# A recurrent scan with mixture-of-experts routing: where row scatters wait, how many expert tiles are known early, and when their outputs are summed

## The chip, the cores and the metric

The kernel runs on one core of one Trainium2 chip. The metric is the device time of one execution in microseconds (us), the median of several runs. A core has five engines that run their own instruction streams and meet only at semaphores: TensorE (PE in the profile; PEld is its weight load), VectorE (DVE), ScalarE (ACT), GpSimd (POOL) and SyncE (SP), which here only issues transfers.

## What is computed

Two blocks on x, of shape (32, 128, 128): batch, time, features.

```python
h = scan(h*(1-alpha) + sigmoid(h@Wh.T + z_t@Wz.T + b)*z_t -> tanh)      # gated scan over 128 steps
x = x + attention(h)                                                    # 16 heads, relative embeddings
h_t = tanh(x_t @ Wx + b + h_{t-1} @ Wh)                                 # second scan over 128 steps
p = softmax(h @ router_w.T); w, idx = top_k(p, 2); w = w / (w.sum() + 1e-9)
out = sum_k w_k * (gelu(h @ w1[idx_k].T + b1[idx_k]) @ w2[idx_k].T + b2[idx_k])
x = x + out                                                             # 8 experts, hidden width 512
```

The change concerns the second scan, the routing and the experts. Each of the 4096 tokens (32 x 128) goes to two of eight experts.

## The kernel before

After the first scan and the attention comes a block that runs the second scan, the routing and the experts.

**The scan.** The 128 steps are cut into NCH = 8 chunks of TC = 16. Iteration m of `chunks` scans chunk m and routes chunk c = m - 1. In step j TensorE waits for the state before (s_h2), multiplies it by Wh (`column_products`, 8 instructions at L420, raising s_r) and then does side work: input sums of the next chunk, the output projection, router logits (steps 5, 9, 13 and 1 of the next chunk), the states' rows (steps 2 to 5) and positions (step 7). ScalarE waits for s_r and takes the tanh (L1125), raising s_h2. This is a closed ring of two engines.

**The routing.** From logits and positions VectorE finds for each token and choice a slot in a list sorted by expert (`choose`, `state_rows`, `slots`, `weights`) and raises s_slot. GpSimd then scatters the rows of the chunk to their slots in the tensor expert_inputs: 2 x JT = 8 indirect transfers (k = 0 to 7) of 128 rows each (L1195 in `scatter`). `scatter_step(c, k)` is the step of the scan at which transfer k of chunk c is due; before each, GpSimd waits for `scatter_step(c, k) + 1` on s_h2, which starts at 1, so for the state of the step ahead. Transfers whose step lies behind the scan (chunk 6, k = 3 to 7: `behind_scan`) and the eight of chunk 7 are issued between expert tiles, at the tiles that `scatter_tiles` names: 0 to 4, and 8, 9, 11, 12, 14, 15, 17, 18.

**The tiles.** The sorted list is worked off in NS = 71 tiles of 128 rows. SyncE loads a tile's rows (`load`, L948, eight buffers RX, each free again when the tile eight before has been written back). TensorE turns them (`turn`, L1079), VectorE copies the columns (L1421), TensorE multiplies by the expert's first weights (`up`, L1086), ScalarE applies the gelu (L1143), TensorE multiplies by the second weights (L1107), VectorE adds the bias (L1471), and GpSimd scatters the tile's 128 output rows to expert_outputs (L1203). ScalarE (L1152) and VectorE (L1427) copy the expert's weights ahead. Sums are double buffered.

Which expert a tile belongs to comes from a table. The first NA = 3 * RX = 24 tiles are full and known from the counts after CA = 4 chunks: VectorE's `early_table(0)`, (1), (2) run behind the routing of chunks 3, 4 and 5, and TensorE's `table_rows(0)` in step 13 of the iteration that routes chunk 5. The others follow from all counts (`late_table`, during tiles 8 to 13). Before SyncE loads tile NA it waits until every row scatter has landed. The first UNROLLED = 24 tiles are written out, the others run in a loop of eight on TensorE, ScalarE and GpSimd.

**The sum over choices.** From tile COMBINE = 44 on VectorE adds, in each tile, one piece (`combine`, two instructions at L1439) of a chunk's two weighted choices to the residual rows; four pieces are a chunk. SyncE loads a chunk's outputs (L957) behind `load(loaded_behind(c))` and stores the finished rows (L961) behind `load(stored_behind(c))`. Pieces that are left when the tiles end run behind the last tile, then chunk 7's weights and its own sum.

Of the kernel before, what the change touches and what calls it, by code (L numbers as in the profile page):

```python
# [14 lines left out]
T = 128  # L15
# [25 lines left out]
def build(nc, a):  # L41

    with ExitStack() as ctx:
# [794 lines left out]
        RX = 8  # L839
        CA = 4  # L840
        NA = 3 * RX
        NB = NS - NA
# [35 lines left out]

        UNROLLED = SPREAD + RX

        def over_tiles(eng, step, late=None):
            for i in range(UNROLLED // RX):
                if late and i == SPREAD // RX:
                    late()
                for k in range(RX):
                    step(i, k, i * RX + k, True, True)
# [11 lines left out]
        s_out = sem("output_written")  # L898
        COMBINE = 44

        def loaded_behind(c):

            return max(tiles_until(c) - 1 + RX, COMBINE + 2 + 2 * c)

# [3 lines left out]

        assert all(COMBINE + JT * c >= loaded_behind(c) - RX + 6 for c in range(NCH - 1))

# [5 lines left out]
        def scatter_step(c, k):  # L916

            return (c + 1) * TC + 10 + 2 * k

        behind_scan = [(NCH - 2, k) for k in range(2 * JT) if scatter_step(NCH - 2, k) >= T]  # L920
        scatter_tiles = dict(enumerate(behind_scan))
        scatter_tiles.update((RX + k + k // 2, (NCH - 1, k)) for k in range(2 * JT))
        assert len(behind_scan) < RX and scatter_step(NCH - 3, 2 * JT - 1) < T

        with nc.Block() as block:
            @block.sync
            def _(sp):
# [12 lines left out]
                for o in range(2):  # L940
                    sp.wait_ge(s_sc[o], CA // 2 * 16 * 2 * JT)

# [51 lines left out]
            def _(pe):  # L994

                def step(m, scan_on, route_on):
# [5 lines left out]
                    for j in range(TC):  # L1002
# [44 lines left out]
                        if j == 7 and scan_on:  # L1047
                            positions(c, 4, 0)
                        if j == 13 and scan_on and c == CA + 1:
                            table_rows(0)  # L1050
# [124 lines left out]
            def _(pool):  # L1175
# [5 lines left out]
                def step(m, scan_on, route_on):  # L1181
# [6 lines left out]
                    for k in range(2 * JT):  # L1188
                        if scatter_step(c, k) < T:
                            pool.wait_ge(s_h2, scatter_step(c, k) + 1)  # L1190
                            scatter(c, k)
# [24 lines left out]
            def _(dve):  # L1216
# [155 lines left out]
                def step(m, scan_on, route_on):  # L1372
# [10 lines left out]
                    for part in range(3):  # L1383
                        slots(c, 4, 0, part)
                    weights(c)
                    count(begun[:, c + 1, :], 0, ALU.is_gt, lambda op: link(c, op))
                    assert k[0] == VLINKS, k
                    if CA - 1 <= c < CA + 2:
                        early_table(c - CA + 1)
                    if m == 1:  # L1390
# [147 lines left out]
```

## Time and profile before

| what | us |
|---|---|
| median of 3 runs | 727.92 |
| lowest, highest | 723.27, 728.98 |
| the profiled execution, whole | 724.73 |
| its span on the core | 721.8 |
| TensorE busy | 600.0 (83%) |
| VectorE busy | 433.5 (60%) |
| GpSimd busy | 400.9 (56%) |
| ScalarE busy | 392.9 (54%) |

Times in the rows are counted from the start of the span; "us" after the start is the length. In square brackets stands how long the engine had been idle and what ended that.

### The profile page before, as it was taken

How to read it: one execution, taken by the hardware profiler on the slowest of the kernel's cores; microseconds unless marked ns; L12 is line 12 of the kernel's file. 1: busy time of each engine (PE TensorE's matmuls, PEld its weight loads, DVE VectorE, ACT ScalarE, POOL GpSimd, SP SyncE). 2: the span in 40 equal slices, each digit the busy share in tenths (PEclk: the TensorE clock that was granted, in tenths of full speed). 3: DMA queues.
4: the chain of work that ended last, by engine and by line, in shares of the span. 5: the costliest groups of instructions: out<-in, count | busy, mean ns of one | idle time of the engine just before them, and what ended most of it. 6: DMA issues, size and time to landing. Idle time of an engine off the chain costs nothing. (4 is left out here: it accounts for less than half of the span.)

```text
span 721.8 us, 27264 instructions
## 1 busy us (share of the span) xinstructions
PE 600.0 (83%) x10479; PEld 454.4 (63%) x10479; DVE 433.5 (60%) x2041; ACT 392.9 (54%) x1112; POOL 400.9 (56%) x433
## 2 busy tenths in 40 slices
PE   3888888888879989999997857777777788999993
PEld 1565555555667766776675734334445777999993
DVE  1666666666557677677765334555545553456775
ACT  4666666666414545555553523222225656899893
POOL 4445554445338878798777421545443656565552
PEclk9999999999979999999999988555556989999997
DMA  7356655555686766677666024333111222225452
GB/s 254 118 207 228 226 186 210 206 205 196 236 246 186 221 177 184 163 217 199 178 182 208 3 88 152 102 97 102 36 54 32 62 79 68 75 75 175 133 160 98
DMA packets 111943, 108.69 MB, mean 151 GB/s; under 512 B 7136, under 2 KB 85472, under 8 KB 111440
## 3 DMA queue, kind: packets, MB, share of 16 engines
q1 hardware_dynamic: 107120, 97.66, 43.0%
q0 software_dynamic: 4320, 8.89, 3.7%
q8 instruction: 78, 1.28, 0.8%
q10 hardware_dynamic: 384, 0.52, 0.2%
q14 instruction: 41, 0.34, 0.2%
HBM read 59.43 MB, written 45.52 MB: 145 GB/s over the span
## 5 line engine op out<-in xcount | busy, mean ns | idle before, releaser
L515 POOL TENSOR_TENSOR sc<-sc,mx 128x1024 f32<-128x1024 f32 x64 | 121.2, 1899 | 53.2 <-DVE mx L673 53.2
L406 POOL TENSOR_SCALAR QD<-q_all,mask 128x128 f32<-128x128 f32 x126 | 88.8, 717 | 98.0 <-DVE pre L361 94.9
L673 DVE CUSTOM_DVE_ANT_0 sc<-banks,s2t 128x128 f32<-128x128 f32 x512 | 112.0, 286 | 49.6 <-PE banks L566 48.2
L1203 POOL DMA_INDIRECT expert_outputs<-yr,xr x71 | 78.5, 1106 | 67.1 <-DVE yr L1471 33.8
L731 ACT ACTIVATE PT<-banks 128x512 f32<-128x512 f32 x128 | 69.8, 596 | 64.2 <-PE banks L579 64.2
L1195 POOL DMA_INDIRECT expert_inputs<-rows,slotu x64 | 63.5, 992 | 68.5 <-ACT h L1125 49.6
L1143 ACT ACTIVATE hid<-banks,w1b 128x128 f32<-128x128 f32 x284 | 81.0, 368 | 24.6 <-PE banks L1086 17.7
L352 DVE COPY s2stage<-banks 128x512 f32<-128x512 f32 (+1 forms) x90 | 76.6, 852 | 16.5 <-PE banks L253 16.5
L1125 ACT ACTIVATE h<-banks,bias 128x32 f32<-128x32 f32 x128 | 36.8, 288 | 86.4 <-PE banks L420 80.2
L1086 PE MATMUL banks<-xt,w1b 128*128 128x128 f32 x568 | 78.0, 282 | 6.8 <-DVE xt L1421 6.8
L1107 PE MATMUL banks<-w2b,hid 128*128 128x128 f32 x568 | 78.4, 283 | 5.3 <-ACT hid L1143 4.9
L253 PE MATMUL banks<-RK,QD 32*128 32x128 f32 x1024 | 78.5, 454 | 3.9 <-DVE s2stage L352 0.9
L1086 PEld LDWEIGHTS banks<-xt,w1b 128*128 128x128 f32 x568 | 71.3, 197 | 8.4 <-DVE xt L1421 8.4
L1107 PEld LDWEIGHTS banks<-w2b,hid 128*128 128x128 f32 x568 | 71.6, 198 | 6.9 <-ACT hid L1143 5.9
L579 PEld LDWEIGHTS banks<-ident,sc 128*128 128x128 f32 x512 | 56.4, 143 | 28.8 <-issue 13.9
L579 PE MATMUL banks<-ident,sc 128*128 128x128 f32 x512 | 70.9, 283 | 0.0
L219 PEld LDWEIGHTS banks<-hs,wh 128*32 128x32 f32 x1016 | 25.5, 140 | 71.2 <-ACT hs L312 71.2
L420 PEld LDWEIGHTS banks<-h,wh 128*32 128x32 f32 x1016 | 24.8, 133 | 71.7 <-ACT h L1125 54.9
L361 DVE TENSOR_TENSOR_SCAN pre<-xz,gl 128x64 f32<-128x64 f32 x128 | 37.5, 293 | 53.9 <-ACT gl L309 50.7
L420 PE MATMUL banks<-h,wh 128*32 128x32 f32 x1016 | 41.1, 242 | 32.0 <-ACT h L1125 27.6
L253 PEld LDWEIGHTS banks<-RK,QD 32*128 32x128 f32 x1024 | 61.1, 318 | 9.8 <-issue 7.8
L219 PE MATMUL banks<-hs,wh 128*32 128x32 f32 x1016 | 42.6, 251 | 28.9 <-ACT hs L312 25.5
(144 smaller groups left out, 1062.7 us busy)
## 6 DMA issues: line engine op xcount, KB each, us to landing
s_scratch<-s2stage SPq DMA_DIRECT2D x32, 1024.0 KB, 4.8
s2t<-s_scratch SPq DMA_DIRECT2D x64, 512.0 KB, 4.9
xr<-expert_inputs SPq DMA_DIRECT2D x71, 64.5 KB
xz<-in_xz SPq DMA_DIRECT2D x8, 512.0 KB, 5.7
yb<-expert_outputs SPq DMA_DIRECT2D x16, 256.0 KB
w2all<-in_w2b SPq DMA_DIRECT2D x8, 320.0 KB
w1a<-in_w1b SPq DMA_DIRECT2D x8, 258.0 KB
k_all<-in_xT SPq DMA_DIRECT2D x1, 2048.0 KB, 11.2
```

The lines of the kernel that those rows point to most:

```text
L219: mm = pe.matmul(ps[bank][at, lo:hi], w[:, at], moving, start=first, stop=last, tile_position=(0, 32 * c), skip_group_check=True)
L253: mm = pe.matmul(ps[4 + j][:, tl * T:(tl + 1) * T], QD[G % 3][32 * j:32 * j + 32, tl].rearrange("p h b -> p (h b)"), relk_window(j, t), st ...
L352: dve.tensor_copy(stage[G % SETS][:, lo:hi].rearrange("p g q k -> p (g q k)"), banks[:, (4 + lo) * BANK:(4 + hi) * BANK]).then_inc(s_s2c, 1)
L406: op = pool.tensor_scalar(QD[G % 3][:, :, h, :], q_all[:, :, quad(G)].rearrange("p b t -> p t b"), mask[:, h:h + 1], None, ALU.mult)
L515: pool.tensor_tensor(sc[U % RING][:], sc[U % RING][:], mx[U % RING][:].unsqueeze(2).broadcast_to([P, HH, T]), ALU.subtract)\
L579: mm = pe.transpose(blocked[:, j // 2, j % 2], sc[U % RING][:, 4 * x + j, :], ident[:])
L673: op = dve.tensor_tensor_reduce(out=sc[r][:, h, :], in0=ps[2 * (U % 2) + h // 4][:, h % 4 * T:(h % 4 + 1) * T], in1=s2t[r][:, h, :], scale ...
L731: act.activation(pairs[:, 2 * (2 * u + x):2 * (2 * u + x) + 2], ps[4 + x][:].rearrange("p (a r) -> p a r", a=2), ACT.Exp, scale=DH ** -0.5 ...
L1086: mm = pe.matmul(ps[2 + k % 2][:, f * P:(f + 1) * P], w1b[k % 2][:, f * P:(f + 1) * P], xt[k % 2][:], start=True, stop=True)
L1107: mm = pe.matmul(ps[4 + k % 2][:, 0:D], hid[k % 2][:, f, :], w2b[k % 2][:, f * D:(f + 1) * D], start=(f == 0), stop=(f == FC - 1))
L1143: op = act.activation(hid[k % 2][:, f, :], ps[2 + k % 2][:, f * P:(f + 1) * P], ACT.Gelu, bias=w1b[k % 2][:, FF + f:FF + f + 1])
L1203: pool.indirect_dma_start(yg_dram, bass.IndirectOffsetOnAxis(xr[k][:, D:].bitcast(U32), 0), yr[k][:], None).then_inc(s_ys[k], 16)
```

## The change

- CA goes from 4 to 5 and NA from 24 to 32: the early table is made from five chunks and covers 32 tiles. `early_table(0)` moves behind chunk 4, (1) into the routing of chunk 5 between slots and weights, (2) behind it; `table_rows(0)` moves to step 15 of that iteration. SyncE's first wait for row scatters counts five chunks.
- UNROLLED goes from 24 to 32 tiles; ScalarE's wait for the late table stays eight tiles ahead of its end.
- `scatter_step` is one step later (11 + 2k), and the wait is for s_r, the product of that step, instead of s_h2.
- The 13 scatters behind the scan go to tiles 1, 2, 4, 5, 7, 9, 11, ..., 23.
- COMBINE goes from 44 to 50, and with it the tiles at which outputs are loaded (54, 54, 56, 58, 60, 62, 70 instead of 46, 48, 50, 52, 54, 62, 70) and sums stored.

```diff
--- before.py
+++ after.py
@@ -837,8 +837,8 @@
         WEIGHTS_IN = 2 * 16 * E
         VLINKS = 20
         RX = 8
-        CA = 4
-        NA = 3 * RX
+        CA = 5
+        NA = 4 * RX
         NB = NS - NA
         ALINKS = 7
         TLINKS = 16
@@ -876,11 +876,11 @@
         s_w2r = sem("second_weights_ready")
         s_tpass = sem("gpsimd_tile_wait_passed")
 
-        UNROLLED = SPREAD + RX
+        UNROLLED = SPREAD + 2 * RX
 
         def over_tiles(eng, step, late=None):
             for i in range(UNROLLED // RX):
-                if late and i == SPREAD // RX:
+                if late and i == UNROLLED // RX - 1:
                     late()
                 for k in range(RX):
                     step(i, k, i * RX + k, True, True)
@@ -896,7 +896,7 @@
         s_o0 = sem("first_choice_added")
         s_sum = sem("chunk_summed")
         s_out = sem("output_written")
-        COMBINE = 44
+        COMBINE = 50
 
         def loaded_behind(c):
 
@@ -906,7 +906,7 @@
 
             return COMBINE + JT * (c + 1) + RX - 2
 
-        assert all(COMBINE + JT * c >= loaded_behind(c) - RX + 6 for c in range(NCH - 1))
+        assert all(COMBINE + JT * c >= loaded_behind(c) - RX + 4 for c in range(NCH - 1))
 
         def fill(eng, e):
 
@@ -915,12 +915,12 @@
 
         def scatter_step(c, k):
 
-            return (c + 1) * TC + 10 + 2 * k
+            return (c + 1) * TC + 11 + 2 * k
 
         behind_scan = [(NCH - 2, k) for k in range(2 * JT) if scatter_step(NCH - 2, k) >= T]
-        scatter_tiles = dict(enumerate(behind_scan))
-        scatter_tiles.update((RX + k + k // 2, (NCH - 1, k)) for k in range(2 * JT))
-        assert len(behind_scan) < RX and scatter_step(NCH - 3, 2 * JT - 1) < T
+        left_over = behind_scan + [(NCH - 1, k) for k in range(2 * JT)]
+        scatter_tiles = dict(zip((1, 2, 4, 5, 7, 9, 11, 13, 15, 17, 19, 21, 23), left_over, strict=True))
+        assert scatter_tiles[9] == (NCH - 1, 0) and scatter_step(NCH - 3, 2 * JT - 1) < T
 
         with nc.Block() as block:
             @block.sync
@@ -938,7 +938,7 @@
 
                 sp.wait_ge(s_tab, ALINKS)
                 for o in range(2):
-                    sp.wait_ge(s_sc[o], CA // 2 * 16 * 2 * JT)
+                    sp.wait_ge(s_sc[o], (CA + 1 - o) // 2 * 16 * 2 * JT)
 
                 def load(t):
                     i, k = t // RX, t % RX
@@ -1046,7 +1046,7 @@
                                     rows_of(k)
                         if j == 7 and scan_on:
                             positions(c, 4, 0)
-                        if j == 13 and scan_on and c == CA + 1:
+                        if j == 15 and scan_on and c == CA:
                             table_rows(0)
 
                 def states(r, k):
@@ -1187,7 +1187,7 @@
                     pool.wait_ge(s_slot, c + 2)
                     for k in range(2 * JT):
                         if scatter_step(c, k) < T:
-                            pool.wait_ge(s_h2, scatter_step(c, k) + 1)
+                            pool.wait_ge(s_r, scatter_step(c, k) + 1)
                             scatter(c, k)
 
                 def scatter(c, k):
@@ -1382,11 +1382,15 @@
                         state_rows(c, 3, part)
                     for part in range(3):
                         slots(c, 4, 0, part)
+                    if c == CA:
+                        early_table(1)
                     weights(c)
                     count(begun[:, c + 1, :], 0, ALU.is_gt, lambda op: link(c, op))
                     assert k[0] == VLINKS, k
-                    if CA - 1 <= c < CA + 2:
-                        early_table(c - CA + 1)
+                    if c == CA - 1:
+                        early_table(0)
+                    if c == CA:
+                        early_table(2)
                     if m == 1:
                         dve.wait_ge(s_xrow, 16)
                         add_rows(0)
```

## Rows read from the trace of the kernel before

**Rows 1.** Busy time by stretch: the second scan, early tiles, later tiles.
```profile
core 0: us, PE busy (x) PEld busy (x) DVE busy (x) ACT busy (x) POOL busy (x), PEclk, DMA share, GB/s
432.00:552.00 120.00, 88.97 (x2291) 48.44 (x2291) 63.17 (x321) 37.95 (x132) 52.78 (x54) 0.57 0.29 90
552.00:620.00 68.00, 57.01 (x450) 53.83 (x448) 32.67 (x122) 44.12 (x126) 37.80 (x36) 0.91 0.25 64
620.00:710.00 90.00, 87.75 (x780) 87.02 (x779) 59.16 (x192) 80.85 (x230) 51.86 (x47) 1.00 0.42 124
```

**Rows 2.** Chain of waits, 425 to 500 us, shares by engine and line.
```profile
by line: PE banks L420 66.5%; ACT h L1125 15.4%; issue 6.0%; DMA packed<-in_packed 6.0%; another core or an unknown queue 2.5%
```

**Rows 3.** Timeline of ScalarE ahead of the first scatter: start, length, instruction, idle before.
```profile
446.43 0.29 ACT L1125 ACTIVATE h<-banks,bias 128x32 f32<-128x32 f32 x1 [0.39 <-PE banks L420]
447.10 0.29 ACT L1125 ACTIVATE h<-banks,bias 128x32 f32<-128x32 f32 x1 [0.39 <-PE banks L420]
```

**Rows 4.** Timeline of all engines in the scan, steady scatters.
```profile
490.66 0.96 POOL L1195 DMA_INDIRECT expert_inputs<-rows,slotu  x1 [1.03 <-ACT h L1125]
...
490.84 0.29 ACT L1125 ACTIVATE h<-banks,bias 128x32 f32<-128x32 f32 x1 [0.45 <-PE banks L420]
...
491.18 0.33 PE L420 MATMUL banks<-h,wh 128*32 128x32 f32 x8
...
492.00 0.29 ACT L1125 ACTIVATE h<-banks,bias 128x32 f32<-128x32 f32 x1 [0.88 <-PE banks L420]
...
492.57 0.96 POOL L1195 DMA_INDIRECT expert_inputs<-rows,slotu  x1 [0.95 <-ACT h L1125]
```

**Rows 5.** All row scatters: length in ns, shortest, median, longest.
```profile
L1195 POOL DMA_INDIRECT expert_inputs<-rows,slotu x64: 957/960/1472, 447.8 to 609.9; - x64
```

**Rows 6.** Timeline of all engines: the first three scatters of a chunk.
```profile
480.00 0.96 POOL L1195 DMA_INDIRECT expert_inputs<-rows,slotu  x1 [1.46 <-ACT h L1125]
...
480.02 0.33 PE L420 MATMUL banks<-h,wh 128*32 128x32 f32 x8
...
480.60 0.29 ACT L1125 ACTIVATE h<-banks,bias 128x32 f32<-128x32 f32 x1 [0.63 <-PE banks L420]
...
481.21 0.69 DVE L1227 TENSOR_TENSOR x1r<-x1r,packed 128x512 f32<-128x512 f32 x1
481.26 1.47 POOL L1195 DMA_INDIRECT expert_inputs<-rows,slotu  x1 [0.30 <-issue]
482.81 0.29 ACT L1125 ACTIVATE h<-banks,bias 128x32 f32<-128x32 f32 x1 [1.93 <-remote]
...
483.56 0.29 ACT L1125 ACTIVATE h<-banks,bias 128x32 f32<-128x32 f32 x1 [0.46 <-PE banks L420]
...
484.12 0.96 POOL L1195 DMA_INDIRECT expert_inputs<-rows,slotu  x1 [1.38 <-ACT h L1125]
485.41 0.29 ACT L1125 ACTIVATE h<-banks,bias 128x32 f32<-128x32 f32 x1 [1.57 <-PE banks L420]
```

**Rows 7.** Timeline of all engines: scatters in a run, early tiles.
```profile
559.42 0.96 POOL L1195 DMA_INDIRECT expert_inputs<-rows,slotu  x1 [0.30 <-issue]
...
560.69 0.96 POOL L1203 DMA_INDIRECT expert_outputs<-yr,xr  x1 [0.30 <-issue]
...
561.95 0.96 POOL L1195 DMA_INDIRECT expert_inputs<-rows,slotu  x1 [0.31 <-issue]
...
563.80 1.14 ACT L1143 ACTIVATE hid<-banks,w1b 128x128 f32<-128x128 f32 x4 [1.86 <-remote]
...
564.22 1.16 PE L1086 MATMUL banks<-xt,w1b 128*128 128x128 f32 x8 [1.61 <-DVE xt L1421]
```

**Rows 8.** Chain of waits in order of time: the last row scatter's landing.
```profile
609.93 2.35 DMA expert_inputs<-rows,slotu
```

**Rows 9.** Timeline of VectorE behind the last tile.
```profile
710.19 0.73 DVE L1439 SCALAR_TENSOR_TENSOR x1r<-yb,wts,x1r 128x128 f32<-128x128 f32 x2
...
717.20 2.44 DVE L1439 SCALAR_TENSOR_TENSOR x1r<-yb,wts,x1r 128x128 f32<-128x128 f32 x8 [4.99 <-DMA yb<-expert_outputs]
```

## Prediction

> **What bounds the kernel now.** I read the busy time by stage first [rows 1]. The change touches three stages: the second scan (432 to 552 us), the expert tiles while GpSimd still scatters routed rows (552 to 620), and the remaining tiles with the sum over choices (620 to 710). The scan is not short of an engine: TensorE shows 89 of 120 us, but at a granted clock share of 0.57, so mostly at 1.2 of its 2.4 GHz. Its 128 steps take 120 us, 0.94 us each. The chain of waits over its first half [rows 2] says what a step is: TensorE's product (L420), then the tanh on ScalarE (L1125), then the next product. So the scan ends when 128 round trips have ended, and anything that makes one trip longer is paid in full.
>
> How long is a trip when nothing disturbs it? Before the first scatter, two states in a row start 0.67 us apart, ScalarE idle 0.39 between them [rows 3], although TensorE has its side work there too. Once scatters run, the steady pattern is another [rows 4]: a scatter starts at 490.66; the state at 490.84 comes on time (idle 0.45, a trip of 0.74 at the lower clock); its successor's product starts at 491.18, yet its state starts only at 492.00, 0.82 behind the product where 0.40 is normal (490.84 less 490.44, the product's start one 0.74 trip earlier). The product is held for 0.42 us. The next scatter comes at 492.57, so two trips take 1.91 instead of 1.48: 0.43 per scatter. The scatter itself lasts 0.96 [rows 5].
>
> At the beginning of a chunk it is worse [rows 6]. Scatter one starts at 480.00, and the product that starts 0.02 later is turned into a state at 480.60, 0.58 behind instead of 0.40: held 0.18. Scatter two is already released and follows 0.30 behind, 481.26 to 482.73; the state after 480.60 comes at 482.81, 2.21 later where 0.74 is normal: held 1.47. Scatter three at 484.12 holds the next one, 485.41 less 483.56 being 1.85: held 1.11. With five steady ones the chunk loses 0.18 + 1.47 + 1.11 + 5 x 0.43 = 4.9 us, against 16 trips of 0.74 = 11.8. That sum, 16.7, is near the spacing of the chunks.
>
> In the tiles one period is 1.91 us: 47 output scatters in 90 us with TensorE busy 87.75 [rows 1]. There TensorE is the bound and nothing is to be won. Between 552 and 620 GpSimd issued 36 scatters, 13 of them routed rows, so 23 tiles were finished in 68 us; 23 x 1.91 is 44, so 24 us are lost, some 5 of them filling the pipeline. Where they go: output and row scatters in a run [rows 7]. Three of a run of four stand there, 559.42, 560.69, 561.95, each 0.30 behind the last (the fourth, an output scatter, ran just ahead of them); ScalarE gets its next sums only at 563.80, 0.9 after the run, and TensorE, out of work, restarts at 564.22 after 1.61 idle. As in the scan, TensorE's finished work is learned of late while GpSimd issues. The stretch's clock, 0.91, costs up to 0.09 x 68 = 6 more. The gate in front of tile 24 shows last: the last row scatter is issued at 609.93 and takes 2.35 to land [rows 8], but it was due at tile 18 and GpSimd was itself behind by then, so I put the gate alone at about 1 us.
>
> **The change, part by part.** (1) The wait of the scan's scatters. Their count stays: steps 11 + 2k instead of 10 + 2k leave the same three of chunk 6 inside the scan, 51 in all. Before, a scatter waited for the state of the step ahead of its own and started 0.27 after that state's end, 0.56 after its start. Now it waits for its step's product, whose signal also starts the state; with the same 0.27 latency it starts about 0.25 after the state's start. The state takes 0.29 and the next product starts 0.05 behind it, 0.34 behind the state's start. So the product at risk starts about 0.09 after the scatter, where it started 0.22 before (passing) and 0.52 after (held) in [rows 4]. The nearest row for +0.09 is the first scatter of a chunk, +0.02, held 0.18 [rows 6]. The following product would start at 0.09 + 0.74 + 0.2 = 1.0, behind the scatter's end at 0.96. I take 0.25 per scatter: bounds 0 (it slips through) and 0.9 (held to where the held ones are let go, 492.00 - 490.66 = 1.34 after the scatter's start, against 0.49 undisturbed). Steady ones gain 5 x (0.43 - 0.25) = 0.9 per chunk.
>
> The first of a chunk cannot start before its slots are known; that is about where it starts today. The second now waits for a product two steps on, some 1.7 us behind the first's start, so it starts some 0.7 us behind the first's end instead of 0.30. The collision goes, and the third's with it: 0.18 + 1.47 + 1.11 - 3 x 0.25 = 2.0 per chunk. Together 2.9 per chunk; 51 scatters are 6.4 chunks: 18.6. Not every chunk is as bad as the one in [rows 6], so I take 16. Behind the waiting scatter only other scatters are queued on GpSimd; their readers (SyncE's loads) come far later.
>
> The SBUF page of the Trainium skill (Who interferes with whom) says that only the port pair shared by VectorE and GpSimd causes contention, TensorE and ScalarE never waiting on anyone. The second scatter of [rows 6] agrees with its other half (1.47 long under a two-input VectorE operation at 481.21, against 0.96), the 0.42 of [rows 4] does not; by the rule alone part (1) is worth nothing.
>
> (2) Table after five chunks. The same VectorE operations, in three other places; the table's product moves from step 13 to 15 of iteration 6. Its values are now computed in that same iteration: about ten small operations of 0.2 to 0.4 us behind the slots. If they are late, TensorE waits in the chain, at most about 1 us once. The first tiles are loaded some 2 us later, 13 us ahead of their use. I take 0.
>
> (3) 32 tiles ahead of the gate, row scatters to tile 23. The gate is then passed eight tiles behind the last row scatter, 15 us against 2.35 for landing: it costs nothing, 1 us won. The spreading wins less than it seems. GpSimd needs 37 issues for tiles 0 to 24 either way; from tile 5 on it is three issues in two tiles, 3 x (0.96 + 0.30) = 3.78 against 2 x 1.91 = 3.82: no gap is left, and runs form again. Fewer pairs stand close (1, 2, 4, 5 at the start, none later, where 8, 9, 11, 12, 14, 15, 17, 18 were). I take one or two stalls of 1.6 fewer less a new one, net 2 won. Bounds: 8 lost (a stall of 1.6 every fourth issue, with no rest in tiles 5 to 7 as before) and 14 won (all but the fill and the low clock). Unrolled code for 32 instead of 24 tiles: TensorE, ScalarE and GpSimd fetch it while they run; 0.
>
> (4) Combination from tile 50. Six more combination steps lie behind the last tile. Each is 0.73 [rows 9], 4.4 us; VectorE sits idle 4.99 there waiting for the last outputs, so they fit with 0.6 to spare. If the cover were gone they would cost those 4.4. At its start chunk 0's outputs are loaded four tiles ahead instead of six: 3.8 us less; VectorE may wait up to 1 us at tile 50. I take 0, range 0 to 2.
>
> Sum: -16 (scan), -1 (gate), -2 (spread) = -19 us. The profiled execution took 724.7 us with a span of 721.8; the median of the runs is 727.9, 3.2 higher. Against the median this gives 709.
>
> **Rivals.** *A, the hold per scatter does not depend on where it starts.* For it: held products appear in nearly every pair. Against it: 490.84 on time and 480.60 late by only 0.18. Then only the collisions go, 1.47 + 1.11 + 0.18 - 3 x 0.43 = 1.5 per chunk at most, and as all chunks are not alike about 6; with 3 from the tiles, -9: 719. *B, slower: the product that starts just behind a scatter is held for the whole issue.* For it: 482.81 and 485.41 [rows 6], let go only about 1.3 to 1.5 after their scatter's start. The price is 0.9 instead of 0.43 for 36 steady scatters (17) less what is saved at the collisions (2.76 - 2.7, nothing): +17 - 3 = +14: 742. It decides from a hold of about 0.68 per scatter: 51 x (0.68 - 0.62, today's mean 4.9 / 8) cancels the 3 us of the tiles. *C, the tiles become one unbroken run.* For it: the 3.78 against 3.82 above. Then (3) costs 8, and with 8 to 16 won in the scan the whole is about -4: 724. *D, the scan by the skill's rule:* nothing in part (1), -3 from the tiles: 725. Against it stands the 0.42.
>
> **How the numbers follow.** Forecast 0.50 (range 700 to 717), A 0.17, B 0.17, C 0.10, D 0.06. About 1%, 7 us, is what a measurement can tell from no change. Faster by more: nearly all of the forecast, most of A, a little of C: 0.64. Within 1%: 0.17. Slower: B and a little of C: 0.19. The range, 699 to 734, leaves out the worse half of B and the tail of the forecast, where the clock would rise too: at the upper level a trip is 0.67 and not 0.74, up to 9 us more.
>
> **What would show it.** Right: the 120 us of the scan near 104; scatters starting about 0.25 behind a state's start; states in a chunk without a gap of 1.9. Wrong: ScalarE idle 1.3 behind every scatter (B). For the tiles: SyncE no longer waits for row scatters; GpSimd's issues 0.30 apart over tiles 5 to 23 with TensorE stalls of 1.6 between them say C. For the end: VectorE's idle time behind the last tile falls from 4.99 to about 0.6.

## The result and the profile after

| | kernel before | changed kernel |
|---|---|---|
| median, us | 725.06 (719.49 to 728.98, 12 runs) | 728.55 (725.76 to 732.21, 12 runs) |
| ratio, 95 % interval | 1 | 1.0075 (1.0055 to 1.0095) |
| profiled execution, whole / span | 724.73 / 721.8 | 728.32 / 726.1 |

The change makes the kernel 0.75 % slower, 3.5 us, where 709 us was forecast: 16 us below the median of the kernel before in this table, 19 below the 727.9 that the forecast started from. The busy time by stretch has the same columns and the same stretches as [rows 1].

```profile
432.00:552.00 120.00, 83.71 (x2202) 46.36 (x2194) 62.77 (x320) 35.09 (x127) 48.85 (x52) 0.57 0.27 84
552.00:620.00 68.00, 55.98 (x484) 50.95 (x484) 31.91 (x118) 42.63 (x120) 35.59 (x35) 0.94 0.23 62
620.00:710.00 90.00, 87.36 (x765) 86.98 (x766) 54.24 (x173) 80.34 (x230) 50.93 (x46) 0.98 0.40 119
```

In the scan's 120 us the trace shows 2202 matmuls of TensorE where it showed 2291: the scan has slowed down. The two tile stretches hardly differ. How long the scan is can be read from the line of its states (first and last start of the 128 tanh instructions), here of the kernel before and of the changed one:

```profile
L1125 ACT ACTIVATE h<-banks,bias x128: 287/288/288, 428.2 to 549.6; 128x32 f32<-128x32 f32 x128
```
```profile
L1125 ACT ACTIVATE h<-banks,bias x128: 287/287/288, 426.7 to 552.5; 128x32 f32<-128x32 f32 x128
```

121.4 us before, 125.8 after: 4.4 us lost where 16 were to be won. What happened to a single scatter is read as in [rows 4], from the timeline of ScalarE, TensorE and GpSimd. First the pattern that is now the commonest, of the changed kernel:

```profile
492.09 0.29 ACT L1125 ACTIVATE h<-banks,bias 128x32 f32<-128x32 f32 x1 [0.45 <-PE banks L420]
...
492.33 0.96 POOL L1195 DMA_INDIRECT expert_inputs<-rows,slotu  x1 [1.32 <-PE banks L420]
492.43 0.34 PE L420 MATMUL banks<-h,wh 128*32 128x32 f32 x8
...
493.67 0.29 ACT L1125 ACTIVATE h<-banks,bias 128x32 f32<-128x32 f32 x1 [1.18 <-PE banks L420]
...
494.41 0.29 ACT L1125 ACTIVATE h<-banks,bias 128x32 f32<-128x32 f32 x1 [0.46 <-PE banks L420]
```

The scatter starts 0.24 behind its state and the product at risk 0.10 behind the scatter, as the prediction worked out (0.25 and 0.09). But this product's state starts only at 493.67, 1.24 behind it and 1.34 behind the scatter: held 0.84. It isn't the data of the transfer that stands in the way. By stretch (columns as in [rows 1]: the scatter's own 0.96 us, then until the state starts, then the next 0.63), the DMA engines move nothing before the state has started:

```profile
492.33:493.29 0.96, 0.86 (x23) 0.31 (x16) 0.67 (x2) 0.16 (x2) 0.96 (x1) 0.50 0.00 0
493.29:493.67 0.38, 0.00 (x0) 0.00 (x0) 0.38 (x2) 0.00 (x1) 0.00 (x0) 0.50 0.00 0
493.67:494.30 0.63, 0.29 (x12) 0.29 (x16) 0.49 (x3) 0.29 (x1) 0.00 (x0) 0.50 0.32 105
```

The same kernel also shows the case that was forecast:

```profile
507.01 0.29 ACT L1125 ACTIVATE h<-banks,bias 128x32 f32<-128x32 f32 x1 [0.46 <-PE banks L420]
507.25 0.96 POOL L1195 DMA_INDIRECT expert_inputs<-rows,slotu  x1 [1.41 <-PE banks L420]
507.35 0.34 PE L420 MATMUL banks<-h,wh 128*32 128x32 f32 x8
...
507.86 0.29 ACT L1125 ACTIVATE h<-banks,bias 128x32 f32<-128x32 f32 x1 [0.56 <-PE banks L420]
...
508.68 0.29 ACT L1125 ACTIVATE h<-banks,bias 128x32 f32<-128x32 f32 x1 [0.54 <-PE banks L420]
```

Same 0.10, held 0.11 and then 0.08, two trips in 1.67. In 42 of the scan's scatters the product starts 0.10 to 0.12 behind: 25 are held 0.80 to 0.95, 16 at most 0.16, one 0.56. Which of the two comes goes for the most part by the scatter's place in its chunk: the fourth is held long in all six chunks, the second and third in none of eleven cases (the 0.56 is one of these), the fifth in three of six. Two more traces with the same wait, e1 and r1 below, show the fourth held in all twelve chunks, the second and third in two of 22. So the distance of 0.10 alone does not say what a scatter costs.

The next table sorts the 127 distances between two successive states of each trace and sums what each class has above 0.74, the undisturbed trip at the lower clock:

| distance, us | before: count, excess | changed: count, excess |
|---|---|---|
| up to 0.8 | 75, -1.1 | 64, -1.1 |
| 0.8 to 1.1 | 9, 1.4 | 29, 3.6 |
| 1.1 to 1.4 | 33, 15.3 | 6, 3.6 |
| 1.4 to 1.9 | 6, 6.0 | 26, 22.8 |
| over 1.9 | 4, 5.9 | 2, 2.9 |

The 33 holds of 0.46 on the mean and most collisions are gone. In their place stand 29 light ones and 26 of about 0.88. The sum of the excess is 27.4 before and 31.8 after; the difference is the 4.4 us. (Two distances in each trace, 0.6 and 1.1 us of excess, stand ahead of the first scatter.) Split by place in the chunk, the two halves of the forecast come apart: the stretches of a chunk's first three scatters, seven in all, have 14.4 us of excess before and 8.7 after, and a steady scatter costs 0.45 before and 0.77 after. The collisions gave 5.7 us, the 30 steady scatters took 9.6.

The first three scatters of one chunk, of the changed kernel, answer to [rows 6]:

```profile
482.69 0.29 ACT L1125 ACTIVATE h<-banks,bias 128x32 f32<-128x32 f32 x1 [0.45 <-PE banks L420]
482.69 0.96 POOL L1195 DMA_INDIRECT expert_inputs<-rows,slotu  x1 [1.91 <-PE banks L420]
...
484.03 0.29 ACT L1125 ACTIVATE h<-banks,bias 128x32 f32<-128x32 f32 x1 [1.05 <-PE banks L420]
484.27 0.96 POOL L1195 DMA_INDIRECT expert_inputs<-rows,slotu  x1 [0.62 <-PE banks L420]
...
484.92 0.29 ACT L1125 ACTIVATE h<-banks,bias 128x32 f32<-128x32 f32 x1 [0.61 <-PE banks L420]
...
485.77 0.29 ACT L1125 ACTIVATE h<-banks,bias 128x32 f32<-128x32 f32 x1 [0.56 <-PE banks L420]
486.01 0.96 POOL L1195 DMA_INDIRECT expert_inputs<-rows,slotu  x1 [0.79 <-PE banks L420]
...
486.51 0.29 ACT L1125 ACTIVATE h<-banks,bias 128x32 f32<-128x32 f32 x1 [0.46 <-issue]
```

The distances are 1.34, 0.89, 0.85 and 0.74: 0.86 above 0.74 in all, where the same three cost 2.76 before. The collision of this chunk is gone. The chunk isn't the mean of the seven, though: by the split above they lost 2.05 each before and lose 1.25 now, so 0.8 was won per chunk. Its first scatter is held 0.60, not 0.25: it starts with the state, and the product 0.33 behind it.

In the tiles GpSimd's issues stand nearly as rival C had them, in runs of three and not in one unbroken run. Timeline of GpSimd, changed kernel:

```profile
597.41 0.95 POOL L1203 DMA_INDIRECT expert_outputs<-yr,xr  x1 [1.91 <-DVE yr L1475]
598.67 0.95 POOL L1195 DMA_INDIRECT expert_inputs<-rows,slotu  x1 [0.30 <-issue]
599.93 0.99 POOL L1203 DMA_INDIRECT expert_outputs<-yr,xr  x1 [0.30 <-issue]
602.84 1.16 POOL L1203 DMA_INDIRECT expert_outputs<-yr,xr  x1 [1.92 <-DVE yr L1475]
```

A run of three, a gap, a run of three: two tiles in 5.43 us where 3.82 is TensorE's pace. One row scatter costs 1.6 us here. From the output scatter of tile 0 to that of tile 24 it takes 64.4 us before and 65.3 now, 24 x 1.91 being 45.8: 1.4 and 1.5 us for each of the 13 row scatters, spread or not. In the run that starts at 597.41 both readers of TensorE's sums are late, not ScalarE alone:

```profile
599.37 1.06 PE L1107 MATMUL banks<-w2b,hid 128*128 128x128 f32 x8
600.38 1.06 PE L1086 MATMUL banks<-xt,w1b 128*128 128x128 f32 x8
601.66 1.14 ACT L1143 ACTIVATE hid<-banks,w1b 128x128 f32<-128x128 f32 x4 [1.80 <-PE banks L1086]
601.76 0.29 DVE L1475 TENSOR_TENSOR yr<-banks,w2b 128x128 f32<-128x128 f32 x1 [1.67 <-PE banks L1107]
```

VectorE takes up its sums 2.39 behind the product's start; without row scatters it is 1.09 (643.34 to 644.43). TensorE, which waits for ScalarE, is idle 1.43 us ahead of its next product at 602.86. The gate costs nothing now. SyncE's wait for row scatters (waits of SyncE from 552 to 640 us: total, times, longest), before and after:

```profile
SPq L967 <- DMA expert_inputs<-rows,slotu: 6.9, 1, 6.9
```
```profile
SPq L967 <- DMA expert_inputs<-rows,slotu: 1.0, 1, 1.0
```

VectorE's tail answers to [rows 9]; the combination pieces that were pushed back run as one group of 14 where VectorE waited 4.99 before, and 0.96 of that wait is left:

```profile
714.68 4.63 DVE L1443 SCALAR_TENSOR_TENSOR x1r<-yb,wts,x1r 128x128 f32<-128x128 f32 x14
...
721.56 0.61 DVE L1443 SCALAR_TENSOR_TENSOR x1r<-yb,wts,x1r 128x128 f32<-128x128 f32 x2 [0.96 <-DMA yb<-expert_outputs]
```

### The profile page after: what moved, and what is told of

Same layout as the page of the kernel before. It is cut to its first block and busy times, and to the rows that moved or that the text cites. A ratio compares the mean times of both kernels' runs of the same rounds, so it can differ in the third digit from the quotient of the medians.

```text
span 726.1 us, 27221 instructions
## 1 busy us (share of the span) xinstructions
PE 599.2 (83%) x10479; PEld 455.2 (63%) x10479; DVE 434.2 (60%) x2041; ACT 392.0 (54%) x1112; POOL 397.0 (55%) x433
## 5 line engine op out<-in xcount | busy, mean ns | idle before, releaser
L1203 POOL DMA_INDIRECT expert_outputs<-yr,xr x71 | 76.8, 1081 | 69.4 <-issue 34.8
L1195 POOL DMA_INDIRECT expert_inputs<-rows,slotu x64 | 61.8, 966 | 75.9 <-PE banks L420 71.3
```

The source lines that it names most:

```text
L1203: pool.indirect_dma_start(yg_dram, bass.IndirectOffsetOnAxis(xr[k][:, D:].bitcast(U32), 0), yr[k][:], None).then_inc(s_ys[k], 16)
```

## The experiments

The theory after the result: while GpSimd makes an indirect transfer, the signal of a finished TensorE product arrives late at ScalarE; how long it is held depends on where in the transfer's making it falls, and the change has moved it to a place where it is mostly held to the end. The rivals: the other edits (tiles, table, combination) cost the time; GpSimd being busy at all is what holds; a scatter that is released by a product is held whatever its phase. "Phase" is how far the product at risk starts behind the scatter's start. The experiments ran on four chips, and each ratio is against the kernel before on the same chip: e1, e2, e4 and e5 on one, e3, e6, e7 and e8 on a second, r1, r2, r3 and e9 on a third, e10 to e13 on a fourth. Where the scan's length is compared with 121.4, that is the first trace of the kernel before; each kernel has one trace.

### One part alone: the wait, and all the rest

```diff
 e1_wait_only (kernel before with)
-            return (c + 1) * TC + 10 + 2 * k
+            return (c + 1) * TC + 11 + 2 * k
-                            pool.wait_ge(s_h2, scatter_step(c, k) + 1)
+                            pool.wait_ge(s_r, scatter_step(c, k) + 1)
 e2_rest_only: the changed kernel with these two lines as before
```

> The kernel before with one part of the change alone: scatters of the scan at steps 11 + 2k, waiting for the product (s_r). Theory P (phase): where a scatter starts against the product's end decides how long the product is held; here the product at risk ends 0.44 us behind the scatter's start and is let go either about 0.6 or about 1.35 behind it. Then this alone slows the scan from 121 to about 126 us, and the kernel by 3 to 6 us (ratio 1.004 to 1.008). Rival T (tiles): the loss lies in the tiles, and this alone is within 1 us of the kernel before, or faster by up to 16 as predicted.

> The changed kernel with the scan's scatters as before: steps 10 + 2k, waiting for the state (s_h2). Theory P: the scan is back at about 121 us and the kernel within 2 us of the kernel before, since the tiles changed by only +0.7 us between first and last output scatter in the two traces. Rival T: it is 3 us slower or more, like the changed kernel.

e1: 729.25 us, ratio 1.0077 (1.0052 to 1.0101), scan 427.5 to 552.9, that is 125.4. e2: 724.81 us, ratio 1.0005 (0.9975 to 1.0035), scan 122.8. The two lines in the scan make the whole slowdown, and what was done to the tiles, the table and the combination comes out at nothing taken together. The changed kernel once more, on the third chip:

> The changed kernel once more, beside whatever kernel-before time this call gives. Theory (the hold of TensorE's signals while GpSimd makes an indirect transfer is the cause): if the kernel before takes about 724 us here, the changed one takes 3 to 6 us more and its scan 125 to 126 us, as before; if the kernel before takes about 677 us here and its signals are not held, the changed one is within 2 us of it, since there is no hold to move, and its scan is 87 to 88 us. Rival (the other edits, the spreading among the tiles, cost by themselves): 3 to 5 us slower on either.

730.19 us against 726.41, ratio 1.004 (1.0009 to 1.007); its scan is 126.4. Slower again, by somewhat less.

### Is it the transfer, or GpSimd at work?

```diff
 e4_scan_without: the 51 scatters of the scan are issued behind it, from buffers of their own for each chunk
-                            scatter(c, k)
+                            pass
 e5_memset_instead: the same, and in the scatter's place in the scan (filler is 128 x 1080)
...
+                            pool.memset(filler[:], 0.0).then_inc(s_filler, 1)
```

> The kernel before with no scatter inside the scan: the 51 are issued in one burst behind it, from one rows buffer per chunk; nothing is left out. The whole is some 60 us longer; the scan's own length, first to last state, is what is read. If GpSimd's issues hold the products and nothing else does (theory P), a step is 0.68 to 0.74 us throughout and the scan takes 88 to 96 us instead of 121. Rival S (side work, or the routing's other operations, make the steps long): it stays above 110.

> As the run without scatters in the scan, but at each scatter's place GpSimd clears a scratch tile of 128 x 1080 floats, about 0.96 us as well. If what holds a product is the making of an indirect transfer (theory D), the scan is as short as without scatters, 88 to 96 us. Rival E (any GpSimd instruction of this length does it, or the wait itself): it stays near 121 us, with states late by 0.4 in every second step.

Both leave nothing out, the scatters only stand elsewhere. The kernels take 747.5 and 753.2 us (one execution each), since 51 scatters in a row now stand in front of the tiles; what counts is the scan, which in e2 on this chip took 122.8. The line of the states, e4 and then e5:

```profile
L1125 ACT ACTIVATE h<-banks,bias x128: 287/287/288, 424.6 to 511.9; 128x32 f32<-128x32 f32 x128
```
```profile
L1127 ACT ACTIVATE h<-banks,bias x128: 287/287/288, 426.6 to 515.3; 128x32 f32<-128x32 f32 x128
```

87.3 and 88.7 us. In e5 GpSimd is busy as long as before (51 memsets of 1.0 us), and the states still come 0.68 apart in the midst of it (timeline of e5):

```profile
479.13 6.58 POOL L1194 MEMSET filler_tile<- 128x1080 f32 x6 [1.89 <-DVE slotu L1367]
...
480.64 0.29 ACT L1127 ACTIVATE h<-banks,bias 128x32 f32<-128x32 f32 x1 [0.39 <-PE banks L420]
...
481.32 0.29 ACT L1127 ACTIVATE h<-banks,bias 128x32 f32<-128x32 f32 x1 [0.39 <-PE banks L420]
...
482.00 0.29 ACT L1127 ACTIVATE h<-banks,bias 128x32 f32<-128x32 f32 x1 [0.39 <-PE banks L420]
```

So it is the indirect transfer that holds TensorE's signals, and since the hold at 492.43 was over before any of its data moved, it is the making of it or what follows the making ahead of the first data. A GpSimd that writes SBUF for as long holds nothing. What is held is only TensorE's word to its readers: from a state's start to the next product's it is 0.34 in 126 of the 128 steps of the changed kernel, as in e4, so ScalarE's word to TensorE is on time. The hold ends later than the making by the profile: in the long cases the state starts 1.3 to 1.45 behind the scatter's start, which lasts 0.96. The 34 us between 121.4 and 87.3 are the 27.4 of the table above and 6.7 of the clock: the granted clock is 0.98 (0.57 before), nearly all at 2.4 GHz, and a trip 0.68 and not 0.74.

### A chip without the hold

The next four kernels ran on another chip, on which the kernel before takes 677.53 us (674.08 to 685.27) instead of some 725.

```diff
 e3_state_one_later (kernel before with)
-            return (c + 1) * TC + 10 + 2 * k
+            return (c + 1) * TC + 11 + 2 * k
 e6_product_and_pause: e1, and ahead of each scatter of the scan (filler is 128 x 8, some 0.05 us)
...
+                            pool.memset(filler[:], 0.0).then_inc(s_filler, 1)
 e7_one_product: the side work's products of the scan in one piece, in six places like
-            return column_products(pe, m % 2, lo * B, (lo + n) * B, w,
+            return whole_product(pe, m % 2, lo * B, (lo + n) * B, w[:],
 e8_left_over_at_once: the five scatters left over behind the scan, in one run ahead of the first tile
...
+                for left in behind_scan:
+                    scatter(*left)
```

> The kernel before with the steps 11 + 2k but still waiting for the state (s_h2). It separates the two halves of the edit. Theory P: a scatter keeps its old start, 0.56 us behind a state's start, so the steady hold stays 0.43 to 0.5 per scatter, and the collision of the first two scatters of a chunk goes: a chunk of 15.5 to 16 us instead of 16.3, the scan 115 to 119 instead of 121, the kernel 2 to 6 us faster than before. Rival Q (the later step itself is what costs, e.g. because side work differs at odd steps): the scan is near 125, the kernel 3 to 6 us slower, as with the product's wait.

> Steps 11 + 2k and the product's wait, but a small GpSimd memset (128 x 8) stands between the wait and the scatter, so it starts some 0.1 to 0.3 us later. The product at risk then ends 0.15 to 0.35 us behind the scatter's start instead of 0.44. Theory P: at 0.44 it stands on an edge (let go at 0.6 or at 1.35); earlier it slips through or is held 0.2, and the scan is 110 to 118 us, the kernel 3 to 10 us faster than before. Rival: the state of the art at 0.44 has nothing to do with an edge, the scan stays near 125.

> The kernel before with TensorE's side work in the scan as one product over all 128 columns instead of four over 32 each: a quarter of the instructions for the same sums. The scan's own products stay as they are. Theory M: what is late is TensorE's report of finished work, and the more instructions it has issued while GpSimd makes a transfer, the longer it takes to catch up; then the hold per steady scatter falls from 0.48 us to 0.2 or less and the scan by 10 us or more. Rival N: the hold depends only on GpSimd's instruction; it stays 0.45 to 0.5, and the scan changes only by what the side work itself takes longer.

> The kernel before with the five row scatters of chunk 6 that do not fit into the scan issued right behind it, in GpSimd's 8.3 us of idle time ahead of the first output scatter, instead of behind tiles 0 to 4. Theory P: a row scatter among the tiles costs about 1.45 us each (18.9 us lost up to tile 24 for 13), so taking 5 out wins up to 7 us there; in the new place they hold TensorE's reports while the first tiles fill the pipeline, which may cost up to 5. Expected 1 to 6 us faster. Rival: what is lost there belongs to the filling of the pipeline and the clock, not to the scatters: no gain or a loss.

| kernel | median, us | ratio (interval) | scan, us |
|---|---|---|---|
| e3 | 676.92 | 0.9979 (0.9951 to 1.0008) | 87.7 |
| e6 | 677.56 | 0.9997 (0.9972 to 1.0023) | 87.3 |
| e7 | 724.95 | 1.0699 (1.0657 to 1.0741) | 135.7 |
| e8 | 677.03 | 0.9973 (0.9947 to 0.9999) | 89.4 |

Timeline of e3, two scatters 1.26 us apart:

```profile
472.28 0.29 ACT L1125 ACTIVATE h<-banks,bias 128x32 f32<-128x32 f32 x1 [0.39 <-PE banks L420]
472.30 0.96 POOL L1195 DMA_INDIRECT expert_inputs<-rows,slotu  x1 [0.31 <-issue]
...
472.95 0.29 ACT L1125 ACTIVATE h<-banks,bias 128x32 f32<-128x32 f32 x1 [0.39 <-PE banks L420]
...
473.56 0.96 POOL L1195 DMA_INDIRECT expert_inputs<-rows,slotu  x1 [0.30 <-ACT h L1125]
473.63 0.29 ACT L1125 ACTIVATE h<-banks,bias 128x32 f32<-128x32 f32 x1 [0.39 <-PE banks L420]
```

States 0.67 and 0.68 apart through two whole scatters of the usual length: nothing is held. The first tiles gain as well: from the output scatter of tile 0 to that of tile 24 it takes 52 us instead of 64 on a chip with the hold. So these runs can't test what was expected where signals are held, and they say something else: the hold takes the indirect transfers and a chip (or a condition of the chip) that has it; of the four chips of these experiments three have it. Only e7 tells something of its own, a miss: with the side work in undivided products a step is 1.0 us, because the next state's product stands behind 0.8 us of it.

### The two of them on a chip with the hold

```diff
 r2_state_one_later: e3 again;  r3_product_and_pause: e6 again;  e9_later_and_at_once: e3 and e8 together
```

> Scatters wait for states as in the kernel before, but for the state of the step after, so that no scatter stands in the same step as GpSimd's chunk work. Where signals are held: the first three scatters of a chunk lose their collisions (held about 1.5 and 1.15 us before) and the steady ones keep their 0.43 us, so the scan falls from 121.4 by 5 x (1.5 + 1.15 - 2 x 0.45), about 9 us, at most, and at least by nothing if one collision is only replaced by another; I take 2 to 6 us faster. Where signals are not held: no change, within 1 us.

> Scatters wait for products as in the changed kernel, one memset of 8 columns ahead of each, so that each starts some 0.1 us later behind the product. Where signals are held: the product at risk ends 0.436 us behind the start in the changed kernel and is mostly held 0.9 us; 0.1 us later the end comes at 0.33, in front of the edge, so it should pass with 0.15 to 0.2 us, and the scan falls to 115 or less (the 16 us forecast for the change come back in part). Rival (the phase does not decide, product-released scatters are always held): scan stays at 125. Where signals are not held: no change.

> The kernel before with the scatters one step later (state-released) and the few that are left over behind the scan issued at once in one run, in place of one per tile. Where signals are held: the 2 to 6 us of the step move, and in the tiles 0 to 3 us more, since five to seven scatters then stand in one run beside the first tile; the rival has the run hold the first tile's products for some 6 us and end even with the kernel before. Where signals are not held: 0 to 1 us faster.

On this chip the kernel before takes 726.41. r2: 725.84, ratio 0.9997 (0.9971 to 1.0023), scan 124.7, a miss: the third scatter's collision goes, the second's stays, and the steady pairs cost no less. e9: 727.65, ratio 1.0026 (0.9998 to 1.0053), a miss too: tiles 0 to 24 take 59.1 us instead of 64.4, but the first output scatter comes 14.6 behind the last state instead of 8.3, as the expectation's rival said. r3: 726.8, ratio 0.9999 (0.9975 to 1.0022); scan 122.5 beside 126.4 of the changed kernel on this chip. That is a miss by the 115 or less expected, and its rival's 125 didn't come either. A delay of 0.05 us ahead of each scatter has brought the product's start from 0.10 to 0.05 behind the scatter's, and those held long from 25 to 19 of 42.

### Further across the edge

```diff
 e10_pause_longer: as r3 with 128 x 136 in place of 128 x 8 (0.15 us later than e1)
 e11_pause_longest: 128 x 248 (0.25 us later)
 e12_changed_and_pause: the whole changed kernel with 128 x 136
 e13_state_and_pause: the kernel before, scatters released by states of the same steps, with 128 x 600
```

> The scan's part of the change (one step later, released by the product), with a memset of 136 columns (about 0.2 us) ahead of each scatter, so that the product at risk ends some 0.29 us behind the scatter's start in place of 0.436. Theory (the phase decides; a signal at 0.35 or less goes out at 0.58): all of them pass with 0.2 to 0.3 us, a pair of steps takes 1.75 to 1.85 us, the scan 112 to 117 us in place of 125 to 126, and the kernel is 6 to 10 us faster than before. Rival (a scatter released by a product is held whatever the phase): the scan stays at 122 to 126.

> The same with 248 columns (about 0.3 us), the product's end some 0.19 us behind the scatter's start. Theory: the signal goes out at 0.58 still, so it is delayed 0.35 to 0.4, 0.1 more than with 136 columns; the scan is 2 to 5 us longer than there (51 scatters, 0.1 each, less what the next step takes up) and shorter than 121. Rival: 122 to 126.

> The whole changed kernel with the memset of 136 columns ahead of each scatter of the scan. The other edits were neutral by themselves (ratio 1.0005), so this should be within 2 us of the kernel with 136 columns alone: 6 to 10 us faster than before if the phase decides, 3 us slower if it doesn't.

> The kernel before, its scatters released by states as before and at the step of before, with a memset of 600 columns (about 0.6 us) ahead of each, so that the two products around it end at about -0.44 and 0.30 us from its start in place of 0.11 and 0.85. Theory (only the phase counts, not what releases): steady pairs as with 136 columns behind a product, 1.75 to 1.85 us; the collisions of a chunk's first three are other ones, so the scan is 112 to 119 us. Rival (the release from the product, or the memset itself, costs): 121 or more.

| kernel | median, us | ratio (interval) | scan, us | distances of 1.4 to 1.9 |
|---|---|---|---|---|
| before | 726.24 | 1 | 121.4 (first trace) | 6 |
| e10 | 717.94 | 0.9898 (0.9873 to 0.9923) | 114.3 | 8 |
| e11 | 718.78 | 0.9902 (0.9878 to 0.9926) | 115.7 | 2 |
| e12 | 722.47 | 0.9938 (0.9919 to 0.9957) | 120.9 | 13 |
| e13 | 718.54 | 0.9892 (0.9855 to 0.9929) | 114.8 | 8 |

Line of the states, then two scatters in the timeline, both of e10:

```profile
L1127 ACT ACTIVATE h<-banks,bias x128: 287/288/289, 426.8 to 541.1; 128x32 f32<-128x32 f32 x128
```
```profile
517.19 0.29 ACT L1127 ACTIVATE h<-banks,bias 128x32 f32<-128x32 f32 x1 [0.80 <-PE banks L420]
517.22 0.21 POOL L1194 MEMSET filler_tile<- 128x136 f32 x1 [0.47 <-PE banks L420]
517.53 0.34 PE L420 MATMUL banks<-h,wh 128*32 128x32 f32 x8 [0.21 <-ACT h L1127]
517.59 0.96 POOL L1202 DMA_INDIRECT expert_inputs<-rows,slotu  x1 [0.16 <-POOL filler_tile L1194]
...
517.93 0.29 ACT L1127 ACTIVATE h<-banks,bias 128x32 f32<-128x32 f32 x1 [0.34 <-PE banks L420]
...
519.00 0.29 ACT L1127 ACTIVATE h<-banks,bias 128x32 f32<-128x32 f32 x1 [0.78 <-PE banks L420]
...
519.40 0.96 POOL L1202 DMA_INDIRECT expert_inputs<-rows,slotu  x1 [0.16 <-POOL filler_tile L1194]
...
519.98 0.29 ACT L1127 ACTIVATE h<-banks,bias 128x32 f32<-128x32 f32 x1 [0.69 <-PE banks L420]
```

The product starts 0.06 ahead of its scatter. Either it is not held at all and the next one is (517.93, then 1.07 to 519.00), or it is held 0.24 itself (519.34 to 519.98 where 0.40 is normal). Both are cheap, 0.24 to 0.36 for the trip, and the long hold has become rare: 4 of the 41 products at -0.06 in e10, none of the 40 at -0.15 in e11. Nearly as good is e13: scatters released by a state, and at the step of before, but 0.6 us later. The rival by which a scatter released by a product is always held falls with e10, and the one by which only that release helps falls with e13.

Split by place in the chunk as above (excess of the seven stretches of a chunk's first three scatters, and of one steady scatter):

| kernel | first three, us | steady, us each |
|---|---|---|
| before | 14.4 | 0.45 |
| changed | 8.7 | 0.77 |
| r2 | 13.3 | 0.57 |
| r3 | 7.9 | 0.70 |
| e10 | 7.9 | 0.44 |
| e11 | 9.2 | 0.42 |
| e12 | 8.9 | 0.61 |
| e13 | 7.6 | 0.45 |

The pause takes away what the changed kernel loses at the steady scatters, and no more: they cost what they cost before. What e10, e11 and e13 win over the kernel before is won at the collisions.

The phase is not the whole of it. In e13 it wanders from -0.25 to 0.28, and of the 11 products at 0.08 to 0.13, the place where 25 of 42 are held long in the changed kernel, none is. And e12 has 11 of 37 held long at the same -0.06 where e10 has 4 of 41. Between e13 and the changed kernel the steps of the scatters differ (even, not odd), the release and the memset; which of these matters wasn't separated. That a memset stands ahead of the scatter isn't enough, by r3.

e10, e11 and e13 beat the kernel before by 1 %; they can't be told from each other. The changed kernel was not run on this chip. e11's scan is 1.3 us longer than e10's where 2 to 5 were expected. e12, expected within 2 us of e10, is a miss: 4.5 us more, with a longer scan in the profiled run (in two of the seven chunks the second and third scatter collide, with trips of 2.27 and 2.25), 68.5 us from tile 0 to tile 24 where e10 takes 65.2, and runs that lie far apart (717.71 to 730.82). Why the changed kernel profits less from the same pause stays open.

## Why the prediction was wrong

**What bounds the kernel**: right. The scan is a row of 128 trips, the scatters' holds, and the clock that falls with them, are nearly all it has above its undisturbed length, and e4 puts a number on it: 34 us.

**Part (1), where the scatter would start**: right to 0.01 us for 42 of them (0.24 and 0.10 measured, 0.25 and 0.09 forecast).

**Part (1), what a start there costs**: this step failed. "I take 0.25 per scatter" came from one row, the first scatter of a chunk with the product 0.02 behind it, held 0.18 [rows 6]; the upper bound, 0.9, was put aside. The product at 0.10 is held at most 0.16 in 16 cases of 42 and 0.80 to 0.95 in 25. A steady scatter, for which 0.25 instead of 0.43 was forecast, costs 0.77 instead of 0.45. From 0.10 to 0.05 to -0.06 to -0.15 the long holds go 25 of 42, 19 of 42, 4 of 41, none of 40, so the cost isn't a smooth function of the phase; and at 0.10 it is for the most part the place in the chunk that decides which of the two comes. The nearest row was no guide in either respect: it stood at another phase and at another step. A scatter cost (31.8 - 27.4) / 51 = 0.09 more than before on the mean, not 0.31 less.

**Part (1), the collisions**: right in kind, too large in size. In the chunk of [rows 6] they cost 0.86 instead of 2.76, 1.9 won where 2.0 was forecast. But 2.0 for each of 6.4 chunks is 12.8, and the seven chunks won 5.7: the chunk read was worse than the mean (2.8 against 2.05 before), and the first scatter, taken at 0.25, costs 0.60. The sum's cut from 18.6 to 16, for chunks that are not alike, was too small.

**Rival B** is what happened, in part: the product just behind the scatter's start is held for the whole making in 25 of 42 cases. Its price for those, 0.9, was right; its sum, +17 for 36 of them, was too high. It took all steady scatters to be held, and it put the gain at the collisions at nothing, where 5.7 us came. The time lay within the range given, 699 to 734, and 0.75 % slower falls to "within 1%", which had got 0.17, for the sake of C and D. That it lay in the range is luck: a loss of 9.6 us and a gain of 5.7, neither forecast in this size, partly cancel.

**Part (3), the tiles**: -3 forecast, nothing measured (e2: 1.0005; its interval ends 1.8 us below the kernel before). The gate's wait did go (6.9 to 1.0), as said, but runs of three issues with gaps of 1.7 to 1.9 stand over most of tiles 5 to 23, near what rival C's condition, 3.78 against 3.82, said. A row scatter costs 1.4 to 1.5 us on the mean in either spreading. Rival C's price, 8 us lost, didn't come: before, the row scatters had cost about as much.

**Parts (2) and (4)**: nothing speaks against the 0 taken for each; e2 shows only that they and part (3) come to nothing together. The 14 pieces behind the last tile take 4.63 us where VectorE had 4.99 idle.

**Rival D**, the scan by the rule of the Trainium skill: the page "SBUF — State Buffer" (Who interferes with whom) says that "PE and ACT never wait on anyone" and that only the port pair shared by VectorE and GpSimd contends. Its first half does not hold for what a kernel sees here: ScalarE starts 1.24 behind a product beside a scatter where 0.40 is normal, and e4's scan without scatters is 34 us shorter. Its second half agrees: e5's memsets, which write SBUF, disturb no trip of TensorE. What is late here is the start of an engine that waits for TensorE, and the section, which is about ports, doesn't say what happens to that; that no port is behind it isn't shown.

**Still open**: why the same phase lets the signal pass at one step and holds it at another; what in the making of a transfer holds it; and why one chip shows none of it. Between the chips only the timing was seen, not a cause.

## What to carry to other kernels

Where GpSimd issues indirect transfers beside a chain of short TensorE steps, try several places for each issue with respect to the product: here a memset of 0.2 us ahead of it made the difference between 0.8 % slower and 1 % faster, each against the kernel before on its chip. If a cost has bounds far apart and only one row near, look for all cases of its kind in the trace and give the far bound its weight; and take a cost that is multiplied by the number of chunks from all chunks, not from one. The row scatters among the tiles cost about 1.5 us each here, and neither spreading them (e2) nor putting five in one run (e9) made the kernel faster.

## What the hardware showed beyond that

- The hold comes with indirect transfers and not with memsets: trips of 0.68 us beside GpSimd's memsets of 1.0 us each (e5), up to 2.3 beside scatters of 0.96.
- It hits VectorE's waits for TensorE as well as ScalarE's (2.39 us behind a product's start instead of 1.09, changed kernel), and it is over before the transfer's data move.
- It differs between chips: 677.5 us against 725 for the same kernel, with the scan at 87 to 88 us and a granted clock of 0.97 (e3) against 121.4 and 0.57.
- The clock follows the holds and not the scatters. Without scatters in the scan the granted clock is 0.98 and trips take 0.68 (e4), with scatters and no holds 0.97 and 0.68 (e3), with scatters and holds 0.57 and 0.74: of the 34 us that the scatters cost the scan 6.7 are the clock's.
